# Moving VectorE's loop boundary, a second residual buffer and two value products in a two-layer graph transformer kernel

## The reference

```python
h = relu(layernorm(x)); x = x + L0(h, adj)      # 6 heads of 64, masked softmax attention, out projection
h = relu(layernorm(x)); x = x + L1(h, adj)      # 12 heads of 32
# L1: h = feat_in @ W;  th = tanh(h)
#     attn = leaky_relu(th @ w_src + (th @ w_dst).T, 0.2), masked by adj, softmax
#     feat_out = elu(attn @ h + b);  gate = sigmoid(feat_in @ H_w.T + H_b)
#     gate * feat_out + (1 - gate) * feat_in
```

## Time and profile before

| | |
|---|---|
| median of 3 runs | 2003.14 us (2001.0 to 2004.61) |
| profiled execution, its own time | 2003.69 us |
| its span, first to last instruction | 2001.8 us |
| mean granted clock of TensorE, share of full | 0.976 |
| busy: PE, DVE, ACT, POOL | 91%, 68%, 55%, 52% |
| DMA | 46.95 MB, mean 23 GB/s |

### The profile page before, as it was taken

How to read it: one execution, slowest core, us unless ns; L and a number is a source line. 1 busy time by engine, 2 the same in 40 slices (tenths; PEclk the granted TensorE clock), 3 DMA queues, 4 the chain that set the end, 5 groups by cost and what they waited for, 6 DMA issues and landing times.

```text
span 2001.8 us, 36327 instructions
## 1 busy us (share of the span) xinstructions
PE 1818.1 (91%) x10992; PEld 1101.0 (55%) x10992; DVE 1364.5 (68%) x3114; ACT 1098.7 (55%) x2215; POOL 1037.3 (52%) x1287
## 2 busy tenths in 40 slices
PE   6999999999999989999999999999899898999985
PEld 4655746556464564655656465564555645456551
DVE  4667576676767767576775766757677676776747
ACT  4566455655545656455564545645565554565644
POOL 4355455554455545545554555644555445554545
PEclk9999999999999999999999999999999999999998
DMA  4000101000010100101001010010100001000000
GB/s 140 17 7 9 40 5 48 5 16 32 5 48 5 47 0 9 44 5 47 0 13 40 5 48 5 9 39 5 48 5 16 32 5 48 5 32 1 5 28 16
DMA packets 38176, 46.95 MB, mean 23 GB/s; under 512 B 2624, under 2 KB 38080, under 8 KB 38080
## 3 DMA queue, kind: packets, MB, share of 16 engines
q1 hardware_dynamic: 38080, 46.03, 6.9%
HBM read 33.44 MB, written 12.58 MB: 23 GB/s over the span
## 4 chain that ended last, share of the span: by engine, by line
PE 60%; DVE 16%; issue 10%; ACT 10%; POOL 3%; DVEq 1%; DMA 1%; ACTq 0%; POOLq 0%; SPq 0%
PE work L1052 13%; PE score L1052 11%; PE acc L1191 8%; PE acc L1195 7%; ACT arena L553 6%; PE score L1110 5%; PE work L1121 5%; PE acc L1136 4%; DVE arena L836 4%; PE acc L1155 2%; DVE sm L795 2%; PE score L1176 2%; DVE xres L817 2%; DVE hT_lo L772 2%; DVE stats L750 2%
## 5 line engine op out<-in xcount | busy, mean ns | idle before, releaser
L836 DVE SCALAR_TENSOR_TENSOR arena<-score,uqT,adjT 128x512 f32<-128x512 f32 x576 | 392.7, 744 | 102.0 <-PE acc L1195 55.7
L401 POOL TENSOR_SCALAR arena<-arena,rinv 128x512 f32<-128x512 f32 x384 | 285.9, 760 | 292.6 <-DVE rinv L801 292.6
L553 ACT ACTIVATE arena<-sm,nmax 128x512 f32<-128x512 f32 x384 | 273.7, 714 | 192.7 <-DVE nmax L795 191.4
L435 POOL TENSOR_TENSOR arena<-arena,adjT 128x512 f32<-128x512 f32 x192 | 224.0, 1167 | 180.3 <-ACT arena L593 175.9
L795 DVE CUSTOM_DVE_ANT_0 sm<-score,mask 128x512 f32<-128x512 f32 x384 | 247.9, 685 | 84.7 <-PE score L1110 82.7
L1121 PEld LDWEIGHTS work<-ident_f,arena 128*128 128x128 f32 x1536 | 171.4, 144 | 166.4 <-issue 81.8
L1121 PE MATMUL work<-ident_f,arena 128*128 128x128 f32 x1536 | 223.2, 286 | 42.5 <-DVE arena L847 28.6
L1191 PE MATMUL acc<-arena 128*32 128x512 f32 x1536 | 203.8, 602 | 36.6 <-POOL arena L435 19.5
L1136 PE MATMUL acc<-arena,v_tok 128*64 128x512 f32 x768 | 200.0, 613 | 16.0 <-ACT arena L559 16.0
L590 ACT ACTIVATE arena<-score,nqT 128x512 f32<-128x512 f32 x192 | 130.2, 678 | 136.2 <-PE score L1176 131.1
L559 ACT ACTIVATE arena<-work 128x512 f32<-128x512 f32 x192 | 113.0, 588 | 164.6 <-PE work L1121 164.6
(11 more groups left out here) (163 smaller groups left out, 3972.8 us busy)
## 6 DMA issues: line engine op xcount, KB each, us to landing
x_in<-in_x SPq DMA_DIRECT2D x16, 768.0 KB, 6.0
xres<-in_x SPq DMA_DIRECT2D x16, 768.0 KB, 4.7
out_x<-xres SPq DMA_DIRECT2D x64, 192.0 KB, 1.9
adj_u<-in_adj SPq DMA_DIRECT2D x16, 256.0 KB, 2.8
arena<-in_wk SPq DMA_DIRECT2D x1, 576.0 KB, 5.0
arena<-in_wq SPq DMA_DIRECT2D x1, 576.0 KB, 6.1
arena<-in_wv SPq DMA_DIRECT2D x1, 576.0 KB, 7.3
arena<-in_wf SPq DMA_DIRECT2D x1, 576.0 KB, 8.3
```

Of the source, the lines that this page charges most:

```text
L401: nc.gpsimd.tensor_scalar(pr, pr, rinv[:, p, t, i:i + 1], 1.0, ALU.mult, ALU.mult).then_inc(probs_ready, 1)
L435: nc.gpsimd.tensor_tensor(edge[:, (n * HG + HG - 1) % 8], t_ring[:, n % 2], adjT[:, n % TT], ALU.mult).then_inc(last_edge_ready, 1)
L553: nc.scalar.activation(probs[p % 2 * 2 + i][:, t], sm[:, n % NSM], ACT.Exp, scale=-1.0, bias=nmax[:, p, t, i:i + 1], accum_out=rsum[:, p, ...
L836: nc.vector.scalar_tensor_tensor(out=edge[:, (n * HG + j) % 8], in0=score[j][:], scalar=uqT[:, c, q:q + 1], in1=adjT[:, c], op0=ALU.max, o ...
```

## The change

VectorE's second norm becomes a function `norm2` of its own, called once ahead of the loop and then at the end of each turn, so that the branch back lies behind it. The residual input gets its own buffer `xb`; its load now waits for the second norm's statistics instead of the stores, and the bias is added at the end of the steps of the turn before. Value product 0 goes from behind step 5 to behind step 7, value product 1 from behind step 7 into the tail, and value 2 one place later in it; four bank homes change. A group's last head is spread first. In `attention` the copy of tile (1, 3) goes ahead of the ELU work of tile 3, `difference` of tile 3 goes two tiles later, and key product 1 one tile earlier. The denominators' weights keep 3 columns of 32.

```diff
+SPREADS = (3, 0, 1, 2)
-    ("v", 0): 1, ("v", 1): 0, ("v", 2): 1, ("v", 3): 1,
+    ("v", 0): 1, ("v", 1): 1, ("v", 2): 1, ("v", 3): 0,
-    ("fin", 0): 0, ("fin", 1): 1, ("fin", 2): 0, ("fin", 3): 0,
+    ("fin", 0): 0, ("fin", 1): 0, ("fin", 2): 1, ("fin", 3): 1,
-KEY_AFTER = {(2, 1): 1}
+KEY_AFTER = {(2, 0): 1}
+        xb = sb("xb", [P, TT, D])
-        u_den = sb("u_den", [P, TT, NG, HG, DH1])
+        u_den = sb("u_den", [P, TT, NG, HG, NG])
             def load_res(b):
-                sp.dma_start(xres[:], ...)
+                sp.dma_start(xb[:], ...)
             def next_res(b):
-                sp.wait_ge(out_stored, START + (b + 1) * 16 * TT)
+                sp.wait_ge(stat_ready[1], (b + 1) * TT)
             def turn(b, adj_too, x_too):
+                next_res(b)
                 if adj_too:
                     next_adj(b + 1)
                 store(b)
-                next_res(b)
...
 # GpSimd
+            def add_bias(g):
+                pool.wait_ge(res_loaded, 16 * g + 16)
+                for t in range(TT):
+                    nc.gpsimd.tensor_tensor(xb[:, t], xb[:, t], bias_f[:], ALU.add).then_inc(xb_ready, 1)
             def layer2(b, more, more2):
-                pool.wait_ge(res_loaded, 16 * b + 16)
-                for t in range(TT):
-                    nc.gpsimd.tensor_tensor(xres[:, t], xres[:, t], bias_f[:], ALU.add).then_inc(xb_ready, 1)
                 root(b, 1)
...
                 if more:
+                    add_bias(b + 1)
                     for t in range(TT):
                         normalise(b + 1, 0, t)
...
+            add_bias(0)          # start-up, behind norm1(1), ahead of normalise(0, 0, t)
...
 # ScalarE, attention
-                if fin:
-                    elu(g - 1, 3)
                 pT_copy(g, 1, 3)
+                if fin:
+                    elu(g - 1, 3)
...
                 pT_copy(g, 2, 1)
-                pT_copy(g, 2, 2)
                 if more:
                     qk_hi_copy(g + 1, 1, "k")
+                pT_copy(g, 2, 2)
 # ScalarE, layer2
-                        if n == 7:
-                            value(b + 1, 0)
-                        if n == 9:
-                            value(b + 1, 1)
+                        if n == 9:
+                            value(b + 1, 0)
                 if more:
                     exps(b + 1, 0, 0)
                 sums_copy(b, NG - 1)
                 if more:
+                    value(b + 1, 1)
                     exps(b + 1, 0, 1)
...
 # VectorE
             def residual(b, t):
                 filled(dve, b, "out", t)
+                if t == 0:
+                    dve.wait_ge(out_stored, START + b * 16 * TT)
-                ... tensor_tensor(xres[:, t], bank_of(b, "out", t)[:, 0:D], xres[:, t], ALU.add)
+                ... tensor_tensor(xres[:, t], bank_of(b, "out", t)[:, 0:D], xb[:, t], ALU.add)
...
+                pT_copy(g, 1, 3)
                 if fin:
                     positive(g - 1, 3)
-                pT_copy(g, 1, 3)
-                if fin:
-                    difference(g - 1, 3)
                 pT_copy(g, 2, 0)
                 if more:
                     qk_low(g + 1, 0, "k")
                 pT_copy(g, 2, 1)
                 ctx_low(g, 1)
+                if more:
+                    qk_low(g + 1, 1, "k")
                 pT_copy(g, 2, 2)
-                if more:
-                    qk_low(g + 1, 1, "k")
+                if fin:
+                    difference(g - 1, 3)
                 pT_copy(g, 2, 3)
...
-            def layer2(b, more, more2):
+            def norm2(b, more):
                 for t in range(TT):
                     dve.wait_ge(xb_ready, b * TT + t + 1)
                     residual(b, t)
...
                     qk_low(b + 1, 1, "q")
+
+            def layer2(b, more, more2):
                 if more2:
                     norm1(b + 2)
...
+            norm2(0, True)
             with dve.Fori(0, B - 2) as b:
                 layer2(b, True, True)
                 attention(b + 1, True, True)
+                norm2(b + 1, True)
             layer2(B - 2, True, False)
             attention(B - 1, False, True)
+            norm2(B - 1, False)
             layer2(B - 1, False, False)
 # PE
-                    ins = nc.tensor.matmul(acc[1][j * DH1:(j + 1) * DH1], u_den[:, c, g, j],
+                    ins = nc.tensor.matmul(acc[1][j * DH1:j * DH1 + NG], u_den[:, c, g, j],
-                for j in range(HG):
+                for j in SPREADS:
                     spread(b, 0, j)
...
-                        if n == 5:
+                        if n == 7:
                             values(b + 1, 0)
-                        if n == 7:
-                            values(b + 1, 1)
                 if more:
                     scores(b + 1, 0, 1)
+                    values(b + 1, 1)
+                turn_sums(b, 0)
+                if more:
+                    scores(b + 1, 0, 2)
                     values(b + 1, 2)
-                turn_sums(b, 0)
-                if more:
-                    scores(b + 1, 0, 2)
                 turn_sums(b, 1)
```

More of the change, by code:

```diff
@@ L88 @@
              ("feat", 0), ("feat", 1), ("feat", 2), ("tok", 0), ("tok", 1), ("tok", 2), ("tok", 3),
-             ("gate", 0), ("gate", 1), ("uq", 0), ("gate", 2), ("gate", 3), ("q", 2), ("v", 0), ("v", 1)]
-          + both("s", 0, 0) + both("s", 0, 1) + [("v", 2), ("fin", 0)] + both("s", 0, 2) + [("fin", 1)]
+             ("gate", 0), ("gate", 1), ("uq", 0), ("gate", 2), ("gate", 3), ("q", 2), ("v", 0)]
+          + both("s", 0, 0) + both("s", 0, 1) + [("v", 1), ("fin", 0)] + both("s", 0, 2) + [("v", 2), ("fin", 1)]
           + both("s", 0, 3) + [("fin", 2), ("v", 3)] + both("s", 1, 0) + [("fin", 3)])
@@ L328, in load_res @@
             def load_res(b):
-                sp.dma_start(xres[:], x[b].rearrange("(t p) d -> p t d", p=P)).then_inc(res_loaded, 16)
+                sp.dma_start(xb[:], x[b].rearrange("(t p) d -> p t d", p=P)).then_inc(res_loaded, 16)
             def next_x(b):
@@ L586, in last_maxima @@
                 if c == 0:
-                    act.wait_ge(r_spread, b * NH1 + h + 1)
+                    act.wait_ge(r_spread, b * NH1 + g * HG + SPREADS.index(HG - 1) + 1)
                 act.wait_ge(last_edge_ready, START + b * STEPS + max(n - 1, 0))
@@ L816, in residual @@
                 filled(dve, b, "out", t)
-                mark_drained(nc.vector.tensor_tensor(xres[:, t], bank_of(b, "out", t)[:, 0:D], xres[:, t], ALU.add),
+                if t == 0:
+                    dve.wait_ge(out_stored, START + b * 16 * TT)
+                mark_drained(nc.vector.tensor_tensor(xres[:, t], bank_of(b, "out", t)[:, 0:D], xb[:, t], ALU.add),
                              b, "out", t)
@@ L831, in edges @@
                     if c == 0:
-                        dve.wait_ge(r_spread, b * NH1 + g * HG + j + 1)
+                        dve.wait_ge(r_spread, b * NH1 + g * HG + SPREADS.index(j) + 1)
                     if j == 0 and n >= 2:
@@ L1278, in layer2 @@
                             query_key(b + 1, 2, "q")
-                        if n == 5:
+                        if n == 7:
                             values(b + 1, 0)
-                        if n == 7:
-                            values(b + 1, 1)
                 if more:
                     scores(b + 1, 0, 1)
-                    values(b + 1, 2)
+                    values(b + 1, 1)
                 turn_sums(b, 0)
@@ L1288, in layer2 @@
                     scores(b + 1, 0, 2)
+                    values(b + 1, 2)
                 turn_sums(b, 1)
```

## The result

The changed kernel takes 1936.92 us (median of 4 runs, 1936.18 to 1938.44); the kernel before, run beside it, 2003.32 (4 runs, 2001.0 to 2004.61). The ratio is 0.9671, with a 95% interval of 0.9654 to 0.9688: 66 us faster. The forecast was 1944, range 1928 to 1966. The profiled execution took 1938.44, its span 1936.6, its mean granted clock 0.985 (before 0.976).

The account below looks back on a forecast made before the run. PE, busy 91% of the span, and its waits were taken to bound the kernel. Terms of -30.2 - 15.0 - 4.9 - 8 - 3 + 2 gave -59 us, from the median 1944 us, range 1928 to 1966.

Parts of the forecast that it names:

- (a): VectorE's loop boundary: the branch's 2.41 us gap moves from the residual sum to behind query 1, covered there; gain 30.2 us.
- Rivals 1 and 5: Branch stall not covered behind query 1, 1975 us (chance 0.12); gap stays at the residual sum, 1974 us (chance 0.04).
- (b): Residual's own buffer: GpSimd's bias sums fit idle time and the residual sum's new wait on the stores has slack; cost 0.
- (c): Copy of tile (1, 3) ahead of the ELU work: PE's wait for it shrinks, 1.0 us a turn, 15.0 us gained.
- (d): Key product 1 a tile earlier fills PE's 0.35 us wait for the copy; 14 turns, 4.9 us gained.
- (e): Spread order: a group's last head comes 0.7 us earlier, PE's step 4 starts 0.5 us earlier; 8 us gained.
- (f): Value products moved later: steps -1.3 us, tail +1.1 us, net -0.2 a turn, -3 us over 15 turns.
- rival 2: Steps and tail together lose, (f) at +16 instead of -3, or transposes behind the tail miss copies: 1963 us, chance 0.11.
- (g): Denominator products with 3 weight columns: the group of eight keeps its length, set by the moving side; change 0.
- (h): Start-up: first bias sums ahead of the first `normalise` +1.1 us, values sharing a bank +0.8; together +2 once.
- Clock: PE's lower clock after the tail's wait, about 0.95 us a turn: taken as unchanged, bounds -12 and +14 us.
- rival 3: Fewer idle stretches give full clock in more turns, -12 us, and (f) is 8 better: 1924 us, chance 0.10.

Follow-up runs that it names:

- run 1: Old kernel with forty empty instructions put on VectorE ahead of its loop, nothing else moved: 1970.20 us, ratio 0.9818.
- run 2: Changed kernel with VectorE's second norm back at the start of the loop body, the old loop boundary: 1972.47 us, ratio 0.9834 against the old kernel.
- run 3: Changed kernel with the old loop boundary and forty empty instructions on VectorE ahead of the loop: 1939.97 us, ratio 0.9667 against the old kernel.
- run 4: Changed kernel with 160 empty instructions at the start of VectorE's program: 1937.04 us, ratio 0.9659 against the old kernel.
- run 5: Changed kernel with the copy of tile (1, 3) behind the ELU work again, on ScalarE and VectorE: 1951.75 us, ratio 0.9738 against the old kernel.
- run 11: Changed kernel with VectorE's last second-norm shift ahead of the first low part and GpSimd's sums waiting for the shifts: 1913.15 us, ratio 0.9548 against the old kernel.

## Why the prediction was right or wrong

The sum was -59 us, measured -66.4; 1937 lies in the stated range and 7 us under the forecast. That the largest term came out right is in part luck and no test of its mechanism: the sum took the same 30.2 us for a stall that is removed as for one that is moved and covered. By its own steps:

- **(a) Loop boundary.** The size holds: 2.20 us a turn at the old place (2.32 less the 0.12 more that the residual sum now waits for PE's product), 28.6 of 30.2 us. The gap did reach PE fully: in run 1 the gap went and the turn became 2.37 shorter. What failed is the step that takes the gap for the cost of every branch back, so that it would come again at the new place, 2.4 us ahead of `norm1`'s first statistics. The stall was removed, in all 13 turns, and the logits' wait stayed at 2.96 instead of 0.55. Moving the branch isn't what removed it: runs 2 and 3 have the branch at the old place, one with the stall and one without. The other half of the step, that a stall at the new place would be covered, was right as run 4 shows (gap 2.25, rest 0.62; predicted 2.41 and 0.55). Rivals 1 and 5 are both out.
- **(b) Residual buffer.** As predicted, 0. The stores never show in a wait of the residual sum, and GpSimd's bias sums are followed by 2.17 us of idle (predicted 2.13), as its timeline shows:

```profile
978.93 3.91 POOL L468 TENSOR_TENSOR xb<-xb,bias_f 128x384 f32<-128x384 f32 x4
985.02 1.36 POOL L405 TENSOR_SCALAR arena<-arena,rinv 128x512 f32<-128x512 f32 x2 [2.17 <-DVE rinv L808]
```

- **(c) Copy of tile (1, 3).** 1.00 us in the stage table, 0.96 by run 5; predicted 1.0.
- **(d) Key product 1.** 0.58 us instead of 0.35, 8.1 us instead of 4.9; the stage also holds the move of `difference`, and no run parts the two. The step counted only the wait it fills; the other 0.23 lies between transposes and products that show no wait of their own, and what makes it was not tried. The term was mis-sized.
- **(e) Spreads.** 0.72 us at the first step, 0.40 left at the last (the predicted 0.7 and 0.5): 6.4 of 8 us.
- **(f) Values.** Steps -1.18 (predicted -1.3), tail +0.85 (+1.1), net -0.33 (-0.2). Both halves were right, so rival 2 is out. The new wait behind the tail is 1.70 us, predicted 1.6.
- **(g) Denominators.** 0, ratio 1.000.
- **(h) Start-up.** The first residual sum comes 0.98 us later, where +2 was predicted. The end, behind the last residual sum, is 0.7 us longer, for which the prediction had no term. Together 1.7.
- **Clock.** Taken as unchanged, since the wait behind the tail stays about as long (1.91 us before, 1.70 after). It gave 5.4 us in the first thirteen turns, as rival 3 has it, though less than its 12. Turns with a half-clock stretch fell from ten to six, in run 1 to four and in run 11 to none. The length of that wait alone doesn't decide it: it is 1.70 us in the changed kernel, with six such turns, and in run 11, with none. Why a given turn keeps one is not settled.

The terms as measured: 28.6 + 15.0 + 8.1 + 6.4 + 5.0 - 1.7 = 61.4, and 5.4 of clock make 66.8, against 66.4 between the medians and 65.2 between the spans.

**What removes the stall.** In VectorE's compiled program of the old kernel 182 instructions stand ahead of the loop and 334 in it, in run 1 222 and 334, in the changed kernel 216 and 340, in run 2 182 and 332, in run 3 222 and 332, in run 4 376 and 340. Stall and 79 to 81 packets go with 182 and 376, no stall and 15 packets with 216 and 222. The length of the loop and its first operation decide nothing here; the place in the instruction stream does. Shown is that the place decides; the blocks are an inference. The Trainium skill ("Runtime: NRT & Kernel Launch", section Instruction fetch mechanics) has a buffer of 512 instructions refilled in blocks of 256 instructions, and a stall for a taken branch whose target is outside the two pages held. Worked out from these figures of the page, as an estimate, a loop of 332 to 340 instructions stalls if it touches three blocks and not if it touches two. If 53 to 73 instructions that the count doesn't see stand ahead of the program, the old kernel, run 2 and run 4 touch three and the others two; all six programs agree with that, and no run shows those instructions themselves. The prediction took every branch back for a stall; that the loop has fewer than 512 instructions was a sign that it need not be one.

**The shift.** The Trainium skill ("GPSIMD Engine Reference", section Specifications) says that GpSimd contends with VectorE instructions that have two SBUF inputs. The trace agrees: `shift` reads two small SBUF tiles and goes from 0.14 to 0.92 us beside GpSimd's sums, while `hT_lo`, whose one input is in PSUM, takes 0.54 to 0.56 either way.

## What to carry to other kernels

When a gap at a loop's first instruction has nothing to wait for, look at the instruction queue's packets before moving work: a few dozen empty instructions ahead of the loop tell in one run whether it is the loop's place in the instruction stream, and here they brought 36 us with nothing moved. A change of the code's length can bring or take such a stall on its own, so a part's worth is read from stages of a turn and from runs that undo one part, not from the total. When a wait is removed, read the length of the operations in the new chain, call by call: here a 128x1 operation that took six times as long as the call before it led to another engine's work, and holding that engine back gave 0.77 us a turn. Read the kernel before in the same way: there the same operation was as long, and PE's lower clock ahead of it hid what it cost.

## What the runs showed of the hardware

- A branch back cost VectorE 2.2 to 3.0 us in each of 13 turns, or nothing, by the position of the loop in the instruction stream alone; in run 1, where VectorE was on PE's path, PE got the whole gap back. Runs 2 and 4 also have a hitch of 0.41 to 0.59 us, in run 2 some 2 us behind the gap, in run 4 some 7 us ahead of it; that it is a fetch too is not shown.
- A VectorE operation on 128x1 with two SBUF inputs took 0.92 us instead of 0.14 while GpSimd ran 128x384 sums of 1.00 us each, and ended with the sum that was under way when it started: 0.92, 0.32 or 0.96 us by where it started in one.
- Four strips of 3 weight columns take as long as four of 32: 592 ns each, ratio 1.000 over 1536 products.
- A turn without a half-clock stretch behind the tail is 0.8 to 0.9 us shorter in the changed kernel and 0.7 to 1.3 in the old one. The number of turns with one fell from ten in the first thirteen (old kernel) over six (changed) to none (run 11), the last two behind the same wait of 1.70 us.
